# Linear attention with a decision tree: attention outputs turned into features by DMA instead of by TensorE

## The reference

```python
xn = layernorm(x)
# attention, 16 heads of 64
Q = elu(xn @ Wq + bq) + 1;  K = elu(xn @ Wk + bk) + 1;  V = xn @ Wv + bv
KV_t = KV_{t-1} + outer(K_t, V_t);  Ks_t = Ks_{t-1} + K_t       # causal, along the sequence
attn = (Q_t @ KV_t) / (Q_t . Ks_t + 1e-6) @ Wo + bo
# tree of depth 8: 255 gates, 256 leaf probabilities
gate = sigmoid((xn @ Wq_tree.T) @ routers.T)
leaf = product of gate or 1 - gate along each path
tree = leaf @ leaf_values @ Wout.T + Wout_b
out = x + attn + tree
```

## Time and profile before

| | us |
|---|---|
| median of 3 runs | 1233.66 (1233.03 to 1235.53) |
| the profiled execution | 1235.54 |
| its span, first to last instruction | 1233.8 |
| PE busy | 1202.1 (97%) |
| POOL busy | 675.5 (55%) |
| DVE busy | 811.4 (66%) |
| ACT busy | 551.7 (45%) |

### The profile page before, as it was taken

How to read it: one execution, slowest core, us unless ns; L and a number is a source line. 1 busy time by engine, 2 the same in 40 slices (tenths; PEclk the granted TensorE clock), 3 DMA queues, 4 the chain that set the end, 5 groups by cost and what they waited for, 6 DMA issues and landing times.

```text
span 1233.8 us, 48282 instructions
## 1 busy us (share of the span) xinstructions
PE 1202.1 (97%) x21669; PEld 1052.3 (85%) x21669; DVE 811.4 (66%) x2186; ACT 551.7 (45%) x881; POOL 675.5 (55%) x842
## 2 busy tenths in 40 slices
PE   5899999999999999999999999999999999999987
PEld 4789889898988989889898988989889898988967
DVE  4774876757667574875758667574866758667462
ACT  3553552535445253552535445253552535445251
POOL 3475556455554665556455554655556465554550
PEclk9999999999999999999999999999999999999998
DMA  6121211212123121222213122121222213122120
GB/s 230 20 53 36 57 34 45 54 36 54 36 46 53 37 54 36 57 34 45 54 36 54 36 46 53 36 54 36 55 36 45 53 36 54 36 45 36 37 36 19
DMA packets 154654, 58.94 MB, mean 48 GB/s; under 512 B 134081, under 2 KB 152784, under 8 KB 154448
## 3 DMA queue, kind: packets, MB, share of 16 engines
q1 hardware_dynamic: 154448, 55.86, 21.8%
HBM read 14.43 MB, written 8.39 MB: 18 GB/s over the span
## 4 chain that ended last, share of the span: by engine, by line
PE 95%; DVE 2%; ACT 1%; POOL 1%; DMA 1%; issue 1%; SPq 0%; POOLq 0%; DVEq 0%
PE s_pair L705 26%; PE w_pair L705 22%; PE o_pair L717 9%; PE s_pair L717 9%; PE o_pair L814 6%; PE s_pair L778 5%; PE o_pair L828 5%; PE kv_pair L789 5%; PE w_pair L758 5%; PE w_pair L740 2%; DMA ffn_tok<-in_L_ffn_Wout_w_dram 1%; ACT ex L455 0%; ACT ex L458 0%; PE o_pair L705 0%; DVE wk L250 0%
## 5 line engine op out<-in xcount | busy, mean ns | idle before, releaser
L353 POOL TENSOR_SCALAR_AFFINE_SELECT aT<-aT 64x512 f32<-64x512 f32 x256 | 167.7, 655 | 366.0 <-ACT aT L482 357.1
L482 ACT ACTIVATE aT<-s_pair 128x512 f32<-128x512 f32 x128 | 76.4, 597 | 337.6 <-PE s_pair L778 337.6
L705 PE MATMUL w_pair<-xnT,wk 128*128 128x512 f32 x768 | 212.3, 412 | 4.1 <-ACT k_tok L468 2.2
L705 PE MATMUL s_pair<-xnT,wq 128*128 128x512 f32 x756 | 200.9, 401 | 1.4 <-POOL aT L353 1.1
L632 DVE TENSOR_TENSOR snaps<-kv_pair,snaps 128x65 f32<-128x65 f32 x768 | 173.3, 226 | 26.5
L404 POOL COPY k_tok<-k_turned 128x1024 uint16<-128x1024 uint16 x126 | 171.4, 1361 | 29.6 <-POOL aT L353 22.6
L396 POOL COPY k_planes<-kT 128x1024 uint16<-128x1024 uint16 x126 | 131.2, 1041 | 95.1 <-POOL k_tok L404 58.2
L455 ACT ACTIVATE ex<-w_pair,neg_bias 128x512 f32<-128x512 f32 x130 | 89.6, 689 | 189.5 <-PE w_pair L705 189.5
L705 PE MATMUL s_pair<-wv,xnT 128*128 128x512 f32 x648 | 168.5, 394 | 0.1
L458 ACT ACTIVATE ex<-ex 128x512 f32<-128x512 f32 x256 | 161.9, 633 | 8.1
L705 PEld LDWEIGHTS w_pair<-xnT,wk 128*128 128x128 f32 x768 | 134.4, 188 | 36.2 <-ACT k_tok L468 2.7
(11 more groups left out here) (107 smaller groups left out, 1972.1 us busy)
## 6 DMA issues: line engine op xcount, KB each, us to landing
x_in<-in_L_attn_x_dram SPq DMA_DIRECT2D x16, 512.0 KB, 5.1
out_dram<-y_buf SPq DMA_DIRECT2D x32, 256.0 KB, 2.1
k_turned<-k_planes SPq DMA_TRANSPOSE x126, 3.1
stage<-in_L_attn_Wv_dram SPq DMA_DIRECT2D x2, 512.0 KB, 8.0
stage<-in_L_attn_Wk_dram SPq DMA_DIRECT2D x2, 512.0 KB, 9.6
stage<-in_L_attn_Wq_dram SPq DMA_DIRECT2D x2, 512.0 KB, 10.9
stage<-in_L_attn_Wo_dram SPq DMA_DIRECT2D x2, 512.0 KB, 9.4
bv_all<-in_L_attn_bv_dram SPq DMA_DIRECT2D x1, 512.0 KB, 8.6
```

Source lines behind the costliest of these rows:

```text
L353: pool.affine_select(out=part, in_=part, compare_op=ALU.is_ge, fill=0.0, base=0, pattern=[[0, 2 * CH], [1, D]], channel_multiplier=-1).the ...
L482: act.activation(aT[:, n % 2].rearrange("p h c q -> p h (c q)"), s_pair[:, :, 0:CH * D], ACT.Copy).then_inc(s_copied, 1)
L705: last = pe.matmul(dst, l, r, start=i == 0, stop=i == len(steps) - 1)
```

## The change

In 109 of the 128 units (`by_dma`: all but p = 7 and units 0 to 2) the outputs go another way from o_tok to oT:

1. POOL copies o_tok's halves apart into `o_planes`, which lies in leaf_odd (`take_output_apart`), between the masks and the keys' `put_together`;
2. SP issues a DMA transpose into `o_turned`, which lies in gate or xn (`turn_output`), ahead of the keys' transpose;
3. one unit later ACT puts the halves together into `o_full` (`put_output_together`), ahead of the keys' exponential, and rounds the high part behind the queries' exponential (`high_of_turned`);
4. DVE subtracts the high part from o_full as its last work of the unit (`low_of_turned`). o_full and oT lie at one place in SBUF, so the low part overwrites what it is made from.

The remaining 19 units keep the transposes on PE, in bank S1 (W1 at p = 7). Beside that: heads go to S1 and tails to W1; DVE does `norm` ahead of `carry`; the waits on PE stand at other places; the two 64-token halves of every odd tile are swapped in x_in, y_buf and the transposes of xn and leaf, and the columns of oT stand in another order, so each load of x and each store of y is three DMAs.

```diff
+def by_dma(n):
+    return n % PAIRS < PAIRS - 1 and n >= 3
...
     fills = [(("K", keys[1], keys[0]), W0)] if keys else []
-    fills += [(name, W1) for name in head]
+    fills += [(name, S1) for name in head]
     if queries:
         fills.append((("Q", queries[1], queries[0]), S0))
-    fills += [(name, S1) for name in tail]
-    fills.append((("oT", p, g), W1))
+    fills += [(name, W1) for name in tail]
     if p == PAIRS - 1:
-        fills += [(("y", 0, g), O1), (("y", 1, g), S1)]
+        fills += [(("oT", p, g), W1), (("y", 0, g), O1), (("y", 1, g), S1)]
+    elif not by_dma(n):
+        fills.append((("oT", p, g), S1))
...
+            def load_block(g):
+                dst, src, done = x_in[:, g % 2], x_rows[g], x_loaded[g % 2]
+                sp.dma_start(dst[:, 0::2], src[:, 0::2]).then_inc(done, 16)
+                sp.dma_start(dst[0:D, 1::2], src[D:P, 1::2]).then_inc(done, 16)
+                sp.dma_start(dst[D:P, 1::2], src[0:D, 1::2]).then_inc(done, 16)
...
+            def turn_output(n):
+                g, p = divmod(n, PAIRS)
+                sp.wait_ge(o_apart, units_by_dma(n))
...
+                if n >= 5:
+                    sp.wait_ge(o_whole, units_by_dma(n) - 2)
+                sp.dma_start_transpose(o_turned(p), o_planes.rearrange("p s n -> p (s n)")).then_inc(o_turned_in, 16)
...
+                if by_dma(n):
+                    turn_output(n)
                 if n + 3 < UNITS:
                     turn_keys(n + 3)
...
+            def take_output_apart(n):
+                k = units_by_dma(n)
+                pool.wait_ge(o_normed, n + 1)
+                if k > 1:
+                    pool.wait_ge(o_turned_in, 16 * (k - 1))
+                pool.tensor_copy(o_planes, o_tok[:, :, :, :].rearrange("p b t n -> p (b t n)").bitcast(U16)
+                                 .rearrange("p (n s) -> p s n", s=2)).then_inc(o_apart, 1)
+                pool.wait_ge(o_apart, k)
...
+            def put_output_together(n):
+                g, p = divmod(n, PAIRS)
+                k = units_by_dma(n)
+                act.wait_ge(o_turned_in, 16 * k)
+                act.activation(o_full[:, 1, p].bitcast(U16).rearrange("p (n s) -> p s n", s=2),
+                               o_turned(p).rearrange("p (s k) q -> p s (k q)", s=2), ACT.Copy).then_inc(o_whole, 1)
+            def high_of_turned(n):
+                g, p = divmod(n, PAIRS)
+                act.wait_ge(o_whole, units_by_dma(n))
+                act.activation(oT[:, 0, p], o_full[:, 1, p], ACT.Copy).then_inc(oT_hi, 1)
...
+            def low_of_turned(n):
+                g, p = divmod(n, PAIRS)
+                dve.wait_ge(oT_hi, n + 1)
+                dve.tensor_tensor(oT[:, 1, p], o_full[:, 1, p], oT[:, 0, p].bitcast(F32), ALU.subtract)\
+                   .then_inc(o_low, 1)
...
+                norm(n)
                 if n + 1 < UNITS:
                     carry(n + 1)
-                norm(n)
...
+                        if c == 0 and t in (0, PAIRS - 2):
+                            until(o_low, units_by_dma(g * PAIRS + max(t, PAIRS - 3)))
```

More of the change, by code:

```diff
@@ L25, with units_by_dma @@
 W0, W1, S0, S1, O0, O1 = range(6)
+def by_dma(n):
+    return n % PAIRS < PAIRS - 1 and n >= 3
+def units_by_dma(n):
+    return sum(by_dma(m) for m in range(n + 1))
 def unit_fills(g, p, blocks):
@@ L807, in from_state @@
                     h = t % 2 ^ turn
+                    if turn == 0 and t < 2:
+                        until(drained[(O0, O1)[t]], uses_before[n][(O0, O1)[t]])
                     for a in range(2):
@@ L864, in tiled @@
                 if n >= 0:
-                    for bank in (O0, O1):
-                        until(drained[bank], uses_before[n][bank])
                     until(sum_ready, sums_after[n])
@@ L935, in _, with normed, head_ready @@
                 fills = unit_fills(n // PAIRS, n % PAIRS, BLOCKS)
-                first_by_vector = any(bank == W1 and name[0] in ("V1", "xT", "leaf") for name, bank in fills)
+                def normed():
+                    until(o_normed, n + 1)
+                def head_ready():
+                    for kind, i, g in (f for f, _ in fills):
+                        if kind == "xT":
+                            until(xn_ready, g + 1)
+                        if kind == "leaf" and i == 0:
+                            until(leaf_step, (g + 1) * LEVEL_STEPS)
                 def masked():
@@ L941, in masked @@
                         until(a_masked, 2 * n + 4)
-                def whole():
-                    if n + 2 < UNITS:
-                        until(k_whole, n + 1)
                 for name, bank in fills:
```

90 lines of the change are left out of this document (65 added, 25 removed).

## The result

The changed kernel takes 1219.74 us (median of 4 runs, 1219.23 to 1222.28), the kernel before 1233.91 us beside it (4 runs, 1233.03 to 1235.53): a ratio of 0.9889, 95% interval 0.9872 to 0.9906. Forecast were 1229.7 us: the direction and the range (1208 to 1249) hold, the gain is 14.2 us instead of 4, and the time lies outside the 1224 to 1236 that the prediction gave its likeliest case. Over all its runs beside the experiments the kernel before took 1228.8 to 1235.9 us, the shortest at a granted clock of 0.998 to 1.000 and the longest at 0.994 to 0.996, so 2 or 3 us between two kernels are not sure from the times alone.

The account below looks back on a forecast made before the run. PE, busy 97% of the span, was taken to bound the kernel. Removed transposes -54.5, stalls +45, edges +3 and late landings +2.5 gave -4 us, so 1233.66 became 1229.7 us; range 1208 to 1249.

Parts of the forecast that it names:

- likeliest case: The forecast itself, 1229.7 us: PE's busy time falls and nearly all returns as short waits; own range 1224 to 1236, chance 0.42.
- late landings: DMA transposes landing late, up to 5.0 us, in both chains: 2.5 us in all, none at best, 20 at worst.
- What is removed: Four o_tok transposes leave PE in each of 109 units: 0.50 us each, 54.5 us in all.
- p = 0 to 1: Normalisation on DVE waits for POOL's copies, so the next scores wait for qT: 0.5 us a block.
- p = 1 to 3: DVE's low part waits 1.6 us behind POOL's residual and its lateness carries on: 0.9 us a block, 0.4 without the lock.
- p = 6 to 7: DVE takes values ahead of queries, as at p = 2: 0.4 us a block.
- p = 7: The low part loses to POOL's gates by 0.04 us and delays the output fill: 1.2 us a block.
- My first rival: DVE wins the collisions at p = 7 and p = 0: 1210 us; chance 0.25 together with the no-lock rival.
- Edges: More DMA issues at start (0.8) and last store (0.75), units 0 to 2 (1.5), k_whole wait (0): 3.0 us.
- ACT's copy: New copy of 1024 elements ahead of the key exponential: 1.06 us, hidden by 0.35 if the transpose has landed.
- Rival 3: Output transposes land too late for ACT, a quarter of the units lose 0.6 to 1 us: 1252 us, chance 0.18.
- Rival 4: PE's hesitation stays and the lock costs as forecast: +2.5, 1236 us, no measurable change; chance 0.15.

Follow-up runs that it names:

- e6: The changed kernel with the four transposes also issued in each of its 109 units, their result unread: 1238.2 us, ratio 1.0043.
- e12: The changed kernel with the two PSUM banks exchanged back in units 3 and 4 of a block: 1235.5 us, ratio 1.0021.
- e3: The changed kernel with the four normalisations at p = 0 moved behind the values' drain, ahead of the queries': 1215.03 us, ratio 0.9856.
- e1: The changed kernel with low_of_turned reading PSUM bank W1 at p = 0 to 5 (wrong values, for timing alone): 1208.9 us, ratio 0.98.
- e8: The changed kernel with unit 0's low part put off from the end of unit 1 to the end of unit 3: 1208.91 us, ratio 0.9808.
- e4: The changed kernel with queries ahead of the gates at p = 5 and 6, and drained before values at p = 6: 1215.44 us, ratio 0.986.
- e2: The changed kernel with POOL's residual at p = 1 as four instructions in place of one: 1223.24 us, ratio 0.9929.
- e11: The changed kernel with e3, e4, e8 and e10 together, plus the four unread transposes in each of 109 units: 1224.26 us, ratio 0.9936.
- e10: The changed kernel with POOL's gates at a block's end waiting for DVE's low part of unit 6: 1215.44 us, ratio 0.9866.

## Why the prediction was right in direction and short in size

The mechanism was right in kind: PE's work falls, most of it comes back as waits, and the largest of them come from the lock, in which DVE and POOL hold each other up. The size was a quarter of what was measured on the spans (-4 against -15.8). With 2.5 us named as the least that can be told from no change, a forecast of 4 us leaves luck a part in the right direction. The 11.8 us are spread as follows; each piece is a difference of keys' starts in the two traces.

| stretch | forecast | measured |
|---|---|---|
| start and block 0 | +3.3 | -3.4 |
| blocks 1 to 14 | -7.0, late landings +2.5 | -8.8 |
| block 15 to the last output fill | -3.5 | -4.4 |
| the last store | +0.75 | +0.8 |

- **What is removed, 0.50 a unit.** Measured 0.55 (7.39 to 6.84), so 60 us instead of 54.5. The number was nearly right and the reason was not: I took it for the transposes and PE's hesitation at them. They are 0.43 (e6); the 0.12 is the wait for the values' bank, and without the exchange of banks, which I had priced at nothing, none of the 0.55 would have come in units 3 and 4 (e12). I had seen that the transposes hide the values' drain, and used it only for unit 2. That 0.50 lay near 0.55 was luck.
- **p = 0 to 1, 0.5.** Measured 8.47 - (8.35 - 0.55) = 0.67. The trace has it as forecast: in block 7 the first of the four normalisations takes 1.56 us and the others 0.40, until POOL's k_tok copy is through, and PE waits for qT ahead of the scores. What the lock alone costs there stays open, since e3 only moved the meeting to another copy.
- **p = 1 to 3, 0.9.** Measured, on means, 8.32 - (7.44 - 0.55) = 1.43. The place and the lock were right. The wait of the low part was too: its median at p = 1 is 2.26 us, so it waits 1.6. Mis-sized is what the lock costs PE: e1 and e8 take 0.9 back, where I had 0.5, and leave 0.55, where I had 0.4 without the lock. The masks and k_tok's copy start behind the residual, and PE waits up to 1.0 us for k_tok even in the four blocks in which DVE wins; I had k_tok at 0.3.
- **p = 6 to 7, 0.4.** Measured 8.34 - (8.39 - 0.55) = 0.50; the order of values and queries (e4 takes 0.32 back).
- **p = 7, 1.2.** This is the step of a block that failed most. Measured 19.75 - 19.37 = 0.38 on the mean. I had written that neither instruction moves by the change, so that POOL keeps its lead of 0.04 us. Before, it had that lead in all 15 blocks; after, DVE is ahead in 11 of them. Where POOL still wins the unit takes 20.37, 1.0 us more than before, near my 1.2; where DVE wins, 0.13 more. My first rival had it the other way, and named the reason: margins of hundredths.
- **Late landings, 2.5 in all.** Unit 4's mean over its undisturbed 6.84 is 0.25, 3.5 us in 14 blocks. The keys' transposes have a median of 3.2 us, against 3.1.
- **Sum of a block:** stalls 0.67 + 1.43 + 0.25 + 0.50 + 0.38 = 3.2, against 3.0 forecast and 0.17 for landings. Two errors of opposite sign met.
- **Edges, +3.0.** Start and block 0 are 6.7 us of the miss, more than half of it. The forecast charged block 0 with a full block's 3.0 of stalls, although units 0 to 2 have no transposes by DMA and so no lock at p = 1, and 2.3 at the start. Measured in block 0: unit 1 grew from 7.40 to 7.99 us, about the 0.5 that I had for each unit with its transposes in S1 (the scores wait 0.41 us for the low part). But unit 2 fell from 8.87 to 7.99: before, PE stopped there 1.10 us for the masks ahead of the queries' last matmul, and in the changed kernel that wait stands a fill later and stops nothing. I had put nothing down for that; it is read from the traces and was not tried by itself. The keys of the first unit start at 46.12 instead of 47.33, and this 1.2 us is chance of the execution. The rows of the stretch from 25 to 50 us, before and after (the last three columns are granted clock, DMA share and GB/s):

```profile
25.00:50.00 25.00, 21.16 (x272) 17.30 (x273) 17.90 (x40) 13.22 (x22) 10.57 (x10) 0.93 0.03 7
```

```profile
25.00:50.00 25.00, 22.17 (x283) 17.90 (x282) 18.27 (x41) 15.49 (x24) 14.06 (x11) 1.00 0.17 41
```

In the profiled execution of before, the granted clock was 0.50, the lower level of 1.2 GHz, from 28 to 30 us, behind a stop of PE of 1.89 us ahead of the keys at 26.32. The executions of e2 and e11, which share the changed kernel's start, show a fall there too and 10.76 us from the first keys' fill to the second; before has 10.78, and the ten others, at a clock of 1.00 over 25 to 50 us, have 9.56 to 9.62. One us more of the 6.7 is chance as well: unit 0 of block 0 took 9.47 us in the profile of the changed kernel and 10.3 to 10.6 in all eleven experiments, where its normalisation met more of POOL's work (2.83 to 3.20 us for 1.79).
- **ACT's copy, 1.06 taken from wo's copy.** Measured 1.37; the cover was 0.16 us instead of 0.35, and held.

Of the signs named: PE's busy time fell by 40, not 50 (the 436 transposes of e6 bring back 39). Waits for qT stand ahead of the scores of p = 1, but at p = 3 PE waits for k_tok and v_aug ahead of the outer products, and at p = 7 the view shows no wait for qT. The low part's median is 0.68; it is 2.26 at p = 1 (2.83 at worst), and 1.56 at worst at p = 7, as foreseen. Rival 3 (slower through late landings) has its case in unit 4, but 0.25 us a block of it. Rival 4 said that PE's hesitation stays: where only the transposes go and the banks don't, it does, and takes the whole 0.55 (e12).

## What to carry to other kernels

Work removed from the engine that bounds a kernel is worth what stands behind it in the queue: here a wait for a bank's drain was hidden behind four transposes, and only the removal together with a change of bank was a gain. So for each instruction removed, ask which wait it covered, and measure both edits apart. When a vector instruction gets a second SBUF input, look for GpSimd's long instructions in the same unit, and move it or order the two by a semaphore: some 10 us (e8) and some 3.5 us (e10) here. And a lead of a few hundredths of a us, even one that holds in all 15 blocks of the old trace, says nothing of who leads after an edit: price both orders, or fix the order. Last, compare the granted clock of the same stretch before a difference at the edges is given to an edit.
